# A spline feed-forward over 32 raw columns and 32 segment sums for each group of rows, and eight weight triples rounded two stages earlier

## The reference

```python
n_ctrl = max(16, int(2048 * 512 / 128.9))
t = np.linspace(0.0, n_ctrl - 1.0, out_size * in_size)
i = np.clip(np.floor(t), 0, n_ctrl - 2); f = t - i
w = 0.5 * (2*p1 + (p2 - p0)*f + (2*p0 - 5*p1 + 4*p2 - p3)*f**2 + (3*p1 - p0 - 3*p2 + p3)*f**3)
gate = x @ gate_w.T; up = x @ up_w.T
out = (silu(gate) * up) @ down_w.T
```

## Time and profile before

| | |
|---|---|
| median of 3 runs | 2489.67 us (2486.84 to 2491.09) |
| span of the profiled execution | 2493.3 us (no other time of its own is given) |
| PE busy, weight loads, DVE, ACT, POOL | 95%, 52%, 54%, 32%, 29% |
| the experts | about 676 to 941 us |
| the weights' stage | about 1261 to 1315 us |
| the columns' stage | about 1315 to 1595 us |

### The profile page before, as it was taken

How to read it: one execution, slowest core, us unless ns; L and a number is a source line. 1 busy time by engine, 2 the same in 40 slices (tenths; PEclk the granted TensorE clock), 3 DMA queues, 4 the chain that set the end, 5 groups by cost and what they waited for, 6 DMA issues and landing times. The chain is left out here.

```text
span 2493.3 us, 30147 instructions
## 1 busy us (share of the span) xinstructions
PE 2377.4 (95%) x10329; PEld 1284.9 (52%) x10329; DVE 1345.9 (54%) x3448; ACT 786.8 (32%) x2069; POOL 733.4 (29%) x728
## 2 busy tenths in 40 slices
PE   8999999989999998999979999989999899999899
PEld 4455455656356555555555565544444344444454
DVE  5544344126111324667667767676664355555797
ACT  1134344303011113555541010231110255655433
POOL 3655455204100004321133433320000165665200
PEclk9999999999999998999959999889999899999799
DMA  6026200014275533110043222450000321111100
GB/s 193 1 80 227 79 17 8 0 52 135 89 286 207 202 133 87 49 38 30 1 154 129 92 76 101 164 195 6 4 9 5 110 59 46 55 47 29 37 13 15
DMA packets 93678, 203.31 MB, mean 82 GB/s; under 512 B 18580, under 2 KB 37428, under 8 KB 91864
## 3 DMA queue, kind: packets, MB, share of 16 engines
q1 hardware_dynamic: 87384, 188.26, 22.4%
q0 software_dynamic: 6144, 13.13, 1.9%
HBM read 150.45 MB, written 45.94 MB: 79 GB/s over the span
## 5 line engine op out<-in xcount | busy, mean ns | idle before, releaser
L3645 POOL TENSOR_SCALAR a_p<-a_p,a_li 100x257 f32<-100x257 f32 x252 | 188.0, 766 | 110.7 <-DVE a_li L3508 110.7
L633 POOL TENSOR_SCALAR a_shared<-a_shared,a_li 128x361 f32<-128x361 f32 x104 | 131.5, 1265 | 182.7 <-DVE a_li L541 182.7
L3263 PE MATMUL bank<-l_early,a_ctx 128*128 128x512 f32 (+1 forms) x384 | 180.1, 614 | 0.0
L2560 PE MATMUL bank<-s_xT,s_w 128*128 128x400 f32 x512 | 179.2, 504 | 0.8 <-PEq L2757 0.8
L2560 PEld LDWEIGHTS bank<-s_xT,s_w 128*128 128x128 f32 x512 | 98.2, 192 | 77.2 <-issue 4.1
L1853 POOL DMA_INDIRECT a_got<-slots_y,slots_of x32 | 33.7, 1054 | 318.6 <-POOLq L1193 309.8
L3263 PEld LDWEIGHTS bank<-l_early,a_ctx 128*128 128x128 f32 (+1 forms) x384 | 68.8, 188 | 85.0 <-issue 85.0
L313 PE MATMUL bank<-a_wk,a_ctx 128*128 128x512 f32 (+1 forms) x192 | 95.0, 616 | 9.3 <-DMA a_wk<-in_L_xattn_Wk 5.6
L691 ACT ACTIVATE a_shared<-a_shared,a_nm 128x361 f32<-128x361 f32 x104 | 62.1, 597 | 98.9 <-DVE a_nm L535 98.9
L2570 PE MATMUL bank<-f_h,s_w 128*128 128x400 f32 x256 | 90.9, 499 | 0.0
L2629 ACT ACTIVATE f_sg<-bank 128x400 f32<-128x400 f32 x32 | 16.1, 503 | 236.6 <-PE bank L2560 236.6
(11 more groups left out here) (477 smaller groups left out, 4985.1 us busy)
## 6 DMA issues: line engine op xcount, KB each, us to landing
slots_x<-zero SPq DMA_DIRECT2D x4, 4096.0 KB, 27.0
f_triple<-in_L_ffn_triples SPq DMA_DIRECT2D x16, 768.0 KB, 4.3
rounded<-f_triple SPq DMA_DIRECT2D x16, 768.0 KB, 3.3
s_whole<-in_L_ffn_w SPq DMA_DIRECT2D x24, 512.0 KB, 3.9
e_wg<-in_L_ffn_w_gate SPq DMA_DIRECT2D x16, 704.0 KB, 4.5
e_wu<-in_L_ffn_w_up SPq DMA_DIRECT2D x16, 704.0 KB, 6.1
e_wd<-in_L_ffn_w_down SPq DMA_DIRECT2D x16, 512.0 KB, 4.4
e_xg<-slots_x SPq DMA_DIRECT2D x16, 512.0 KB, 5.4
```

The lines of the kernel that those rows point to most:

```text
L633: pool.tensor_scalar(p[s % NP], p[s % NP], li[:, b % 2, h:h + 1], None, ALU.mult).then_inc(normed, 1)
L2560: mm = nc.tensor.matmul(banks[f % 2][:, 0:GT], w[:, kc, f * P:(f + 1) * P], xT[:, kc, :], start=(kc == 0), stop=(kc == KC - 1))
L3263: mm = nc.tensor.matmul(bank[0:m, :], columns[:, kc], w[:, kc, :], start=(kc == 0), stop=(kc == KC - 1))
L3645: pool.tensor_scalar(p[g % 2][j][:, lo:hi], p[g % 2][j][:, lo:hi], li[:, h, i:i + 1], None, ALU.mult) \
```

## The change

**Gate and up.** The 2048 rows are sorted by their phase (how far into its interval a row begins) and cut into 16 groups of 128 rows of like phase. For group g, 32 columns near the interval borders are kept as they are (`own`): 32 rows of contraction against the raw x. All other columns of a segment are a cubic of the column's number, so that x enters only through sums of x times a power, five segments of four powers, and up to 12 more single columns: another 32 rows of contraction against these sums (`moments`). A gate or up product of a group is so two matmuls of 32 rows instead of four of 128. Four groups share the 128 partitions, so that the matmuls of a pair of groups, and of gate and up, lie in four row groups. The blocks are done in pairs: up of a pair is done one step behind its gate, and down two steps behind.

**The weights' stage.** Four parts instead of 12 are built the old way (down only). They are written to HBM (`natural`) and gathered back with their rows in the sorted order by 16 indirect DMAs of POOL. Gate's and up's 32-row weights come from four taps each in HBM times factors, eight tiles each: DVE makes gate's, POOL up's. All 8 batches are normed and turned here, and PE makes the sums of x with a `basis` matrix, 32 matmuls of 128 rows x 400 columns.

**The triples.** The rounding is now a class, `Triples`. Eight of the 16 triples are rounded in the experts' stage, the other eight in the columns' stage, half a triple a pair.

The diff, cut to its core:

```diff
@@ stage_L0_experts
+        triples = Triples(k, ctx, "e0", raw, k.rounded, 0, EARLY_TRIPLES, 3)
                 rows8.sync(sp, *weights8)
+                for t in range(3):
+                    triples.load(sp, t)
                 for e in range(NE):
...
                     store(2 * e + 1)
+                    if 1 <= e <= EARLY_TRIPLES:
+                        triples.store(sp, e - 1)
+                        if e + 2 < EARLY_TRIPLES:
+                            triples.stored(sp, e - 1)
+                            triples.load(sp, e + 2)
...
+                step = Link(dve, stepped)
+                triples.scales(dve, step, 0)
                 product(0)
                 for u in range(U):
                     if u + 1 < U:
                         product(u + 1)
                     result(u)
+                    if u < triples.n:
+                        if u + 1 < triples.n:
+                            triples.scales(dve, step, u + 1)
+                        triples.rounding(dve, step, u)
...
+            @block.gpsimd
+            def _(pool):
+                triples.pool(pool)
@@ class Triples
+    def scales(self, dve, step, n):
+        t = n // 2
+        dve.wait_ge(self.tri_in[t % self.room], 16 * (t // self.room + 1))
+        if n >= 2:
+            dve.wait_ge(self.rounded_made, n - 1)
...
@@ stage_columns_ffn, PE
+                        mm = nc.tensor.matmul(bank[:, 0:GT], weights[w, far][lane, f // 4, :],
+                                              (moments if far else xT)[lane, f // 4, tokens], start=not far, stop=bool(far))
...
+                    gates = range(2 * n, 2 * n + 2) if n < 2 * PAIRS else []
+                    ups = range(2 * n - 2, 2 * n) if n > 0 else []
+                    if n >= 1:
+                        pe.wait_ge(silued, 2 * n)
+                    if n >= 2:
+                        pe.wait_ge(h_made, 2 * n - 2)
+                    for far in range(2):
+                        for m in gates:
+                            part(0, m, far, b_g[m % 2], gate_made)
+                        for m in ups:
+                            part(1, m, far, b_u[m % 2], up_made)
...
-                for n in range(FC):
+                gate_up(0)
+                gate_up(1)
+                for n in range(2, PAIRS + 1):
                     gate_up(n)
-                    if n > 0:
-                        down_part(n - 1)
+                    down_part(2 * n - 4)
+                    down_part(2 * n - 3)
+                project()
+                down_part(FC - 2)
                 down_part(FC - 1)
...
@@ stage_columns_ffn, DVE
+                triples.scales(dve, step, 0)
+                for n in range(2 * PAIRS):
+                    product(2 * n)
+                    product(2 * n + 1)
+                    if n == PAIRS - 1:
+                        dve.wait_ge(all_made, 1)
+                        dve.tensor_tensor(early.all8[:], b_u[1][0:B, :], early.bout[0:B, :], ALU.add).then_inc(all_copied, 1)
+                        for b in range(GB):
+                            add(b)
+                    if n + 1 < triples.n:
+                        triples.scales(dve, step, n + 1)
+                    triples.rounding(dve, step, n)
...
@@ stage_L1_ffn, SP
+                    def load_taps(t):
+                        if t >= 2:
+                            for n in range(2):
+                                sp.wait_ge(taps_used[n], t - 1)
+                        sp.dma_start(by[t % 2][:], w_in["spline_by"][t]).then_inc(taps_in[t % 2], 16)
+                        for n in range(2):
+                            sp.dma_start(taps[n][t % 2][:], w_in["spline_taps"][n, t]).then_inc(taps_in[t % 2], 16)
...
+                    load_part(3)
+                    store_part(0)
+                    load_taps(2)
+                    store_part(1)
+                    load_taps(3)
+                    store_part(2)
+                    load_taps(4)
+                    store_part(3)
+                    for t in range(5, TILES_W):
+                        load_taps(t)
@@ stage_L1_ffn, POOL
+                    for t in range(TILES_W):
+                        up_weights(t)
+                    pool.wait_ge(basis_in, 32)
+                    pool.wait_ge(natural_out, PARTS_W * 16)
+                    for f in range(FC):
+                        pool.indirect_dma_start(wd[:, f, :], None, natural[:, :],
+                                                bass.IndirectOffsetOnAxis(ap=order[:, f:f + 1], axis=0)).then_inc(down_in, 16)
+                    pool.wait_ge(down_in, FC * 16)
@@ stage_L1_ffn, DVE
+                    for t in range(PARTS_W):
+                        measure(2 * t)
+                        measure(2 * t + 1)
+                        beyond_border(t)
+                    for b in range(B):
+                        normalize(b)
+                    for t in range(TILES_W):
+                        gate_weights(t)
```

More of the change, by code:

```diff
@@ L2460, in spline_terms @@
             for r in range(4):
-                out[side, m + side, r] = sum(coef[e][m] * binom[e][r] * (u - side) ** (e - r) for e in range(r, 4))
+                out[side, m + side, r] = sum(CATMULL_ROM[e][m] * BINOMIAL[e][r] * (u - side) ** (e - r) for e in range(r, 4))
     return np.ascontiguousarray(out.reshape(2, TERMS, CHUNK).transpose(1, 0, 2).astype(np.float32))
@@ L2491, in stage_columns_ffn @@
+def stage_columns_ffn(k, tag, weights, down, xT, moments, raw, rounded, early, recurrence):
     nc = k.nc
-    nb = HALF // BLOCK
+    PAIRS = FC // 2
     with ExitStack() as ctx:
@@ L2569, in down_part @@
+                def down_part(m):
+                    f = m % FC
+                    if f == 0 and m > 0:
+                        pe.wait_ge(added, m // FC * GB)
+                    pe.wait_ge(h_made, m + 1)
                     for d in range(KC):
-                        mm = nc.tensor.matmul(b_y[d][:, 0:GT], down[:, f, d * P:(d + 1) * P], h[f % 2][:],
+                        mm = nc.tensor.matmul(b_y[d][:, 0:GT], down[:, f, d * P:(d + 1) * P], h[m % 4][:],
                                               start=(f == 0), stop=(f == FC - 1))
@@ L2692, in add @@
                     dve.tensor_tensor(k.res[:, b, :], k.res[:, b, :], b_y[b % GB][0:S, :], ALU.add).then_inc(added, 1)
-                scales(0)
-                for n in range(2 * FC):
-                    product(n)
-                    if n == FC - 1:
-                        normalize(GB)
-                        normalize(GB + 1)
-                    if n + 1 < 2 * FC:
-                        scales(n + 1)
-                    rounding(n)
-                    if n == 3:
+                triples.scales(dve, step, 0)
@@ L2726, in _ @@
-                for n in range(2 * FC):
-                    pool.wait_ge(inv_made, n + 1)
-                    if n >= 2:
-                        pool.wait_ge(rounded_made, n - 1)
-                    pool.tensor_tensor(blocks(v[n % 2][:]), half(n), over(inv[n % 2]), ALU.mult).then_inc(scaled, 1)
-                    if n >= 1:
-                        finish(n - 1)
-                finish(2 * FC - 1)
-def stage_L1_ffn(k, points, powers, beyond, terms, raw, rounded, early, recurrence):
+                triples.pool(pool)
@@ L2752, in stage_L1_ffn @@
+            var, rstd = sb("var", [S, B]), sb("rstd", [S, B])
+            xn = [sb(f"xn{i}", [S, D]) for i in range(2)]
+            basis, order = sb("basis", [P, KC, FC * 32]), sb("order", [P, FC], U32)
+            by = [sb(f"by{i}", [P, 4, P]) for i in range(2)]
+            taps = [[sb(f"taps{w}{i}", [P, 4, P]) for i in range(2)] for w in range(2)]
             tm = sb("terms", [P, 2, P])
```

424 lines of the change are left out of this document (248 added, 176 removed).

## The result

| | before | after |
|---|---|---|
| median of four runs, us | 2490.38 | 2421.68 |
| range of the runs, us | 2486.84 to 2493.05 | 2420.43 to 2424.22 |
| profiled execution's span, us | 2493.3 | 2418.3 |
| weights' stage, start to start of the next, us | 53.8 | 91.8 |
| columns' stage, start to start of the next, us | 280.0 | 148.5 |

The ratio of the medians is 0.9724, 95% interval 0.971 to 0.9738: faster, by 68.7 us. 2420 was forecast. Stage by stage the trace gives +23.0 (experts), +1.1 (the attention between), +38.0 (weights), -131.5 (columns) and -5.6 behind them: -75.0 for the two profiled executions, whose spans differ by more than the medians.

A forecast was written before the change was run, and what follows sets the result against it. The prediction took PE, busy 95% of the span, as the bound. Columns' -128, weights' +34 and experts' +24 us summed to -70: span 2423, median 2420 us, range 2397 to 2464.

The forecast's parts named there:

- Experts' head: Start of the experts: DVE waits for the late first triple, PE turns its first product at 708.0, not 685.29; +23.8 us.
- 0.94 of credit: Experts' head: PE's later wait of 0.94 us for `e_xg` was to go.
- The rest of the experts at nothing: Experts behind the head: DVE's 6.8 us a unit stay under PE's 8.3; +0 to +16 us, nearest to 0.
- Weights' stage: Late first gate tile, slow tile turns in two places, then 16 gathers; +34 us, from +26 to +46.
- Columns' stage: 279 us become 151 at 7.4 us a pair of blocks; gain 128 us, from 107 to 136.
- DVE's loop: Columns' stage: rounding 4.23, POOL's multiplication back 1.66 and scales 1.42 us, 7.31 us a pair against PE's 7.35.
- six waits of 0.5 us for reloads: Columns' stage: each of six triple reloads lands 0.5 us late, 3 us in all.
- The middle: Middle of the columns' stage: open downs, `project`, `summaries`, turning, adding and rounding take 23.8 us instead of 7.4; +16.4.
- Rival 1: Columns' stage: row groups do not overlap, PE needs 11.2 us a pair, +61 us, total 2481; chance 6%.
- Rival 2: Columns' stage: the clock stays at half, 14.7 us a pair, slower at 2530 us; chance 5%.
- Rival 3: Experts: the head costs nothing because the first triple lands early, total 2396 us; chance 5%.
- Rival 4: Weights' stage: POOL's gathers of 128 scattered rows take double (2.6 us), +21, total 2441 us; chance 14%.

The follow-up runs named there:

- e1_later: Changed kernel with the whole rounding in the experts, with its steps, stores and loads, begun three units later; 2407.89 us.
- e8_all: Changed kernel with the orders of e6 and e7_middle together, experts' rounding begun five units later and triples' loads behind the next experts' loads; 2377.67 us.
- e5_no_round: Changed kernel without any rounding in the columns' stage, its eight triples loaded and stored as they came; 2415.52 us.
- e10_full: Changed kernel with gate and up matmuls of the columns' stage over all 128 rows instead of 32, none overlapping; 2472.83 us.
- e4_one_group: Changed kernel with all 32-row matmuls of the columns' stage on rows 0 to 31, so none overlap; 2538.25 us.
- e2: Changed kernel with only the first triple's load issued ahead of the second expert's and the attention's weights; 2409.22 us.
- e6: Changed kernel with the weights' stage reordered: stores before tap tiles, gate tiles ahead of and between norms, gathers between up tiles; 2405.23 us.
- e7_middle: Changed kernel with `project`, `summaries` and their loads moved to the weights' stage, and silus and gate/up earlier in the columns' middle; 2411.97 us.

## Why the prediction was right

*Experts' head*: forecast +22.7 with PE's turn at 708.0 and, with 2 for the clock and 0.94 of credit, +23.8; measured 22.67 of waiting, 708.08, and +23.0 at the last expert's downs. What the working had not seen is that the same loads hold `e_xg` back as well, by 7 us: a wait that lay inside the first one, so that the sum was right without it, and that cost 8.5 us of what e1_later was to give back. The 2 us for the low clock behind the rest are there: the second turn of mid comes 10.16 us behind the first (718.24), not 8.08. *The rest of the experts at nothing* held: units kept 8.08 us, in e8_all too.

*Weights' stage*: +34 forecast, +38.0 measured. The mechanism was the one forecast, DVE's late first gate tile, slow turns with two places, gathers behind. POOL ended its tiles at 1352.78, which is 24.1 less, or 1328.7, in the frame of before (1325 forecast); the gathers' 1.25 us each (1.31) gave 1 us back; the landing took about 4.4 (2.8). The mis-sized terms are DVE's way to the end of its first gate tile, 1322.3, or 1298.2, against 1296.3 (norms of 1.07 us for 0.9, a tile of 1.70 for 1.4), and the turns of the six tiles behind it, 30.5 us for 28.7. A part of the second is a slip in adding: the terms that the prediction names for a turn make 8.55 us, not 8.2, which is 1 us over three turns.

*Columns' stage*: -128 forecast, -131.5 measured. PE's pair took 7.12 (7.35 forecast): the eight matmuls 1.55 for 1.75, less than the sum that had 0.16 us a round for the change of form in it. The Trainium skill (TensorEngine Tiling (Array Packing), Key Properties) says that a change of tiling mode drains TensorE; whatever it costs is inside these 1.55 us and the 5.64 of the downs. DVE's loop was 7.31, as forecast. That it, at 7.4 with waits, would set the stage's pace was wrong: PE's steps were 7.12 or 7.13 us apart but for two (7.28 and 7.31), and e5_no_round, without the loop, ran no faster outside the middle. The forecast came out all the same, since the two periods are within 0.2 us. The six waits of 0.5 us for reloads were one of 0.56 (7.87 against 7.31). The middle took 26.0 for 23.8: the half clock of the two downs, 2.8 us, was not in the sum. From the last products to the next stage it took 13.1 for 11.3. The upper end that the prediction gives the gain, 136 at 7.0 a pair, is 134 by its own terms; nothing hangs on it.

*Rivals.* Rival 1 did not come; e10_full shows that its price was right. Rival 2 did not come either, and e4_one_group shows it, mechanism and all, once the first is there. That the two hang together was not seen: the prediction priced them apart, at 2481 and 2530; the trace of e4_one_group has both, 2538. Rival 3 did not come: the triple landed late, at 706.1. Rival 4's gathers did not double.

*Behind the columns* 5.6 us were gained that no term holds. The 20 us after the start of that stage ran at another clock (the kernel before, then after):

```profile
1595.20:1615.20 20.00, 19.37 (x72) 13.06 (x73) 15.24 (x37) 9.76 (x18) 10.73 (x12) 0.57 0.59 200
```

```profile
1525.80:1545.80 20.00, 16.70 (x96) 11.80 (x97) 17.68 (x43) 13.84 (x26) 11.83 (x13) 0.91 0.80 267
```

PE had done the same in the 10 us before, at full clock. It is no effect of the change that the runs can show: with the same code there the "rest" of e1, e2, e5, e6 and e7 was 892.3 to 897.1 us and this stretch's clock 0.58 to 0.66, in e8 0.91. In e7_middle, whose rest was the shortest, it was 0.66, so this stretch alone does not carry the difference. What decides it stays open. In part the 5.6 us belong to the two executions that were profiled: the spans differ by 75.0 us and the medians by 68.7, and of the four runs of the changed kernel the profiled one was the fastest (2420.43).

*How close 2420 is* owes something to luck. By spans the forecast was -70 and the result -75.0: 4 us too little for the weights' stage and 3.5 too much left in the columns cancel, and 5.6 us behind them were in no term; the medians moved by 68.7.

## What to carry to other kernels

Work that is put on an idle engine brings its loads along: price the queue that they stand in, for the transfers behind them too, before the engine's time. When one wait is removed, look at what has been hidden inside it. Where a bound falls by more than half, the next ones are close together (here 7.31 and 7.12): read each engine's own starts, since products every 7.31 us did not mean that PE waited for them. A stage that only prepared data becomes worth ordering: 18 us here without leaving anything out.

## What was not expected of the hardware

With PE busy throughout, matmuls of 32 rows in one row group, between full ones, brought the granted clock to 0.70, and the same matmuls over 128 rows kept 1.00; the lower ones cost 65 us more in all (2538.25 - 2472.83), although their rows of the trace are as long at equal clock (0.34 us each). Eight fp32 matmuls of 32 rows x 400 columns in four row groups took 1.55 us against 5.38 without overlap, a factor of 3.5. POOL's multiplication of 128 x 512 took 1.78 us where DVE's of the same tile ran beside it and 1.27 where not.
